# Run sums of a graph kernel copied out of their PSUM banks by ScalarE into four SBUF places, and added from there by VectorE one unit later

## The reference, cut to what matters

```python
h = gelu(x @ W_pre + b_pre)
aggr = segment_sum(h[src] * edge_attr, dst)      # layer 0: gather, weigh, sum by node
x1 = x + aggr
y = gelu(gelu(x1 @ W1 + b1) @ W2 + b2)
x2 = layernorm(x + x1 + y)

t = x2 @ W_lin.T + b_lin                         # layer 1: the same edges, no edge weights
agg = segment_sum(t[src] * dinv[src] * dinv[dst], dst)
out = layernorm(x2 + relu(agg + x2 @ W_root.T + b_root))
```

## Time and profile before

| | |
|---|---|
| three runs | 1155.4, 1145.21, 1153.62 us (median 1153.62) |
| profiled execution | 1145.42 us, span of the trace 1143.6 us |
| busy share PE, DVE, ACT, POOL | 82%, 64%, 44%, 73% |
| mean granted TensorE clock | 0.91 of full speed |

### The profile page before, as it was taken

How to read it: one execution, slowest core, us unless ns; L and a number is a source line. 1 busy time by engine, 2 the same in 40 slices (tenths; PEclk the granted TensorE clock), 3 DMA queues, 4 the chain that set the end, 5 groups by cost and what they waited for, 6 DMA issues and landing times. The chain is left out here.

```text
span 1143.6 us, 20856 instructions
## 1 busy us (share of the span) xinstructions
PE 934.5 (82%) x7455; PEld 811.1 (71%) x7455; DVE 737.3 (64%) x1442; ACT 499.6 (44%) x846; POOL 839.2 (73%) x915
## 2 busy tenths in 40 slices
PE   6744776667667966888989999989999999799796
PEld 6643544444445844776888888789999989698696
DVE  8177987676777677668657858734435465556655
ACT  2303876566755675567557666541001010001116
POOL 7787777777777777777777777777777777777603
PEclk9866987778877988999999999999999999899898
DMA  8542876567666768788899899979998888677734
GB/s 226 158 116 61 301 264 217 188 197 244 193 201 196 241 220 277 219 272 291 267 288 280 252 319 304 300 228 288 275 262 267 253 255 246 183 198 193 183 84 96
DMA packets 185668, 260.24 MB, mean 228 GB/s; under 512 B 68600, under 2 KB 163832, under 8 KB 178968
## 3 DMA queue, kind: packets, MB, share of 16 engines
q1 hardware_dynamic: 158278, 215.57, 58.6%
q0 software_dynamic: 26992, 42.82, 15.9%
q10 hardware_dynamic: 290, 0.45, 0.2%
HBM read 173.12 MB, written 85.62 MB: 226 GB/s over the span
## 5 line engine op out<-in xcount | busy, mean ns | idle before, releaser
L855 POOL DMA_INDIRECT gath<-table_h,srcs x791 | 781.6, 988 | 241.2 <-issue 239.3
L1494 PE MATMUL bank_q<-piece_raw,early_late 128*96 128x250 bf16 x3453 | 407.4, 272 | 7.6 <-issue 3.2
L1494 PEld LDWEIGHTS bank_q<-piece_raw,early_late 128*96 128x96 bf16 x3453 | 380.2, 124 | 12.4 <-issue 5.1
L944 ACT CAST counts_raw<-bank_q 128x490 bf16<-128x490 f32 x400 | 279.6, 756 | 153.3 <-PE bank_q L1472 149.9
L1440 PE MATMUL seg<-onehot,msg 128*97 128x128 f32 (+1 forms) x1662 | 237.0, 296 | 69.5 <-DVE msg L1244 40.4
L1440 PEld LDWEIGHTS seg<-onehot,msg 128*97 128x97 f32 x1662 | 214.5, 183 | 85.5 <-issue 58.7
L1472 PE MATMUL bank_q<-hots_raw 128*128 128x245 bf16 x834 | 161.3, 289 | 49.9 <-ACT counts_raw L944 33.5
L1342 DVE TENSOR_TENSOR hots_raw<-counters,kb 128x1960 bf16<-128x1960 bf16 (+1 forms) x157 | 182.3, 1161 | 0.0
L944 ACT CAST counts_raw<-bank_b 128x490 bf16<-128x490 f32 x200 | 151.4, 757 | 69.3 <-PE bank_b L1472 66.7
L1244 DVE TENSOR_TENSOR msg<-gath,edg 128x480 f32<-128x480 f32 x166 | 108.1, 651 | 96.2 <-DMA gath<-table_h,srcs 87.1
L1472 PEld LDWEIGHTS bank_q<-hots_raw 128*128 128x128 bf16 x834 | 70.7, 103 | 112.9 <-ACT counts_raw L944 69.0
(11 more groups left out here) (196 smaller groups left out, 623.4 us busy)
## 6 DMA issues: line engine op xcount, KB each, us to landing
counts_hbm<-counts_raw SPq DMA_DIRECT2D x50, 1531.2 KB
piece_raw<-counts_hbm SPq DMA_DIRECT2D x250, 250.0 KB
edg<-in_edge SPq DMA_DIRECT2D x166, 240.0 KB
gath<-table_h,srcs POOLq DMA_INDIRECT x791
piece_raw<-counts_hbm SPq DMA_DIRECT2D x38, 125.0 KB
piece_raw<-counts_hbm SPq DMA_DIRECT2D x25, 187.5 KB
counts_raw<-counts_hbm SPq DMA_DIRECT2D x4, 625.0 KB, 5.9
gath<-x_hbm SPq DMA_DIRECT2D x10, 234.4 KB
```

Source lines behind the costliest of these rows:

```text
L855: pool.indirect_dma_start(gath[0:k, u % GS * UT + j, :], None, table[0], bass.IndirectOffsetOnAxis(ap=srcs[0:k, t:t + 1], axis=0)).then_in ...
L944: act.copy(counts[:, k % 2, :, i * WD:(i + 2) * WD].rearrange("p a (w n) -> p w a n", w=2), counted).then_inc(s_kept, 1)
L1494: mm = pe.matmul(sums(r)[0:D, 0:DN], parts[:, FINE[c] + i, part, :], rows, start=(first and i == 0 and part == 0), stop=(last and i == til ...
```

## The change

ScalarE gets a new item `keep`, put right behind the last piece of each run: it waits for the run's last piece and copies the 96x250 sums from the bank into one of four SBUF places `run_sums` (a place is free again when the `dense` of four runs before is done). `begin_run` now waits for that copy (`s_run_kept`) instead of for `dense`. `dense` takes its input from `run_sums`; it is put one unit later (`u - 1`), and up to four runs may wait when a new one begins. In the building stage a new run may begin while others wait. The pieces are the same 313; there are 171 runs instead of 170.

```diff
 def schedule():
         if last:
+            order.append(("keep", r))
             waiting.append((u, r))
     def flush(u):
-        while waiting and waiting[0][0] < u:
+        while waiting and waiting[0][0] < u - 1:
             order.append(("dense", waiting.pop(0)[1]))
     def next_piece(u, least):
-                while len(waiting) > 2:
+                while len(waiting) >= KS:
                     order.append(("dense", waiting.pop(0)[1]))
...
-                if open_run or not (waiting and u <= built + 1):
-                    next_piece(u, next(n for until, n in LEAST if u < until))
+                next_piece(u, next(n for until, n in LEAST if u < until))
...
+        run_sums = sb("run_sums", [D, KS, DN])
...
+            def keep_run(r):
+                act.wait_ge(s_used, runs[r][1] + 1)
+                if r >= KS:
+                    act.wait_ge(s_dense, r - KS + 1)
+                act.copy(run_sums[:, r % KS, :], sums(r)[0:D, 0:DN]).then_inc(s_run_kept, 1)
...
             def dense(r):
-                run_sum = sums(r)[0:D, 0:DN]
+                run_sum = run_sums[:, r % KS, :]
...
-                dve.wait_ge(s_used, q + 1)
+                dve.wait_ge(s_run_kept, r + 1)
...
             def begin_run(r):
                 if run_before(r) is not None:
-                    pe.wait_ge(s_dense, run_before(r) + 1)
+                    pe.wait_ge(s_run_kept, run_before(r) + 1)
```

More of the change, by code:

```diff
@@ L61 @@
 LATER = 1
+KS = 4
 ZS = 4
@@ L456, in build @@
         s_dense = sem("s_dense")
+        s_run_kept = sem("s_run_kept")
         s_taken = sem("s_taken")
@@ L990, in _ @@
                 what = item[0]
+                if what == "keep":
+                    keep_run(item[1])
                 if what == "meta":
@@ L1345, in dense @@
             def dense(r):
-                e, q, is_apart, takes = runs[r]
-                run_sum = sums(r)[0:D, 0:DN]
+                e, _, is_apart, takes = runs[r]
+                run_sum = run_sums[:, r % KS, :]
                 high = upper[:, (e - SPLIT) * DN:(e - SPLIT) * DN + DN] if e >= SPLIT else None
```

## The result

The changed kernel takes 1157.13 us (median of 19 runs, 1151.41 to 1164.4), the kernel before 1148.88 us (19 runs, 1140.82 to 1155.4) on the same chip. The ratio is 1.0084, 95% interval [1.0063, 1.0104]: the change costs 9.6 us, 0.84%. The forecast was 6.3 us or 0.5% slower, "same" within 1%. It gave 1160 us, but from a base of 1153.62 us, the median of three runs; with 19 runs that base is 1148.88 us. So 1160 lies near 1157.13 partly by luck, and the difference of 9.6 us is what has to be explained. Sign and size class came out; the reason came out in part only, and the following is mostly about that.

What follows compares the result with a forecast made beforehand. GpSimd's chain of gathers was taken to bound the kernel. Adds 6.0 us plus copies 0.3, all else 0, gave 6.3 us on 1153.62: 1160 us, range 1150 to 1171 (the forecast case's own 1157 to 1164).

Steps and rivals of the forecast that it cites:

- GpSimd's chain sets the pace: From 110 to 1083 us GpSimd goes from gather to gather, one each 1.28 us; slack at unit 112 is 14.9 us.
- The keeps in the building stage: ScalarE's copies there make TensorE 2 to 12 us late by unit 112; the slack covers it, so 0.
- The adds: 133 dense before unit 162 become adds with two SBUF inputs that delay GpSimd's gathers: 6.0 us, bounds 0 and 16.9.
- The 0.045: Gather delay in us per two-SBUF add, from three hits, 0.49 us together, among 11 L1360 adds before the last gather.
- The rule for an instruction at random: Gather delay from a VectorE instruction of length d: (d - 0.12)^2 / 2.56, giving 0.034 us for 0.416 us.
- The 13 copies: Dense that are copies (L1364, 0.414 us from PSUM) become copies inside SBUF; at half of L1360's price, 0.3 us.
- The tail: Behind unit 162's gathers: chunk 12's t some 1 us earlier, four additions about 2 us later; together 0, bounds -3.6 and +1.5.
- The step that failed: Chunk 12's first step gains three adds (1.8 us); the Gelu's table load behind a keep gives most of that back.
- are hidden in its idle time: After the building stage ScalarE has little to do, so its copies of run sums there cost nothing.
- The last four additions: At the end, four additions stand behind the last add; the last chunk and step1 wait for them, about 2 us.
- 77.4 us from message 162 to the end, within 2: Check set beforehand: unit 162's message to the end of the span stays 77.4 us; if it moves, the prediction is wrong.

Runs made afterwards that it cites:

- The experiment with the adds alone: Kernel before, with dense reading an SBUF tile of zeros in place of the bank, same waits and order: 1148.55 us against 1146.84, ratio 1.0022.

## Why the prediction was right or wrong

**GpSimd's chain sets the pace, and the copies don't stop it.** Right. Its waits for messages are 2.1 us, and the message of unit 112 is earlier: it ends at 761.22 + 0.65 = 761.9 us, its room is needed at 785.48, so the slack grew from 14.9 to 23.6 us. The smallest of all units is now 21.4 us.

**The keeps in the building stage: 0.** Right, and by the reason given. TensorE's new waits for a copy are 6.3 us in 18 cases, the longest 1.4, where 2 to 12 us were worked out; VectorE's waits for pieces are gone, and the kernel with the copies up to unit 150 is 1.0012.

**The adds: 6.0 us.** The mechanism was right, the term too large, by two times or more. The experiment with the adds alone gives 2.5 us (0.5 to 4.7), and the gathers that start under an add run 2.2 us over in its trace and 2.1 in that of the changed kernel, 0.015 us an add, not 0.045. The 0.045 was three hits among eleven. The rule for an instruction at random, 0.034, lay nearer but was too large too; why the adds meet fewer starts than at random is open. *The 13 copies: 0.3 us.* Inside SBUF they take 0.29 us on average and not 0.41; they lengthen two gathers, by 0.02 and 0.06 us.

**The tail: 0, bounds -3.6 and +1.5.** Wrong, and here most of the loss is: 7.9 us by the kernel that copies only from unit 150 on. The step that failed reads "ScalarE's table load before that chunk's Gelu now stands behind a keep, which gives most of that back". It priced one load in one place as less than 1.8 us, where chunk 12's first Gelu comes 3.6 us later behind its product. It left out that the copy itself waits (2.06 us for its piece), that the load before the square root stands behind a copy too, and that chunk 11 has the same two loads and passes its lateness on to message 162. The same holds for its sentence that behind the building stage the copies "are hidden in its idle time". The bound above was worked out from VectorE's additions alone; it should have held the loads, 1.28 us in the four places of chunks 11 and 12, 5.1 us, with the copies' waits on top (one of the four, the square root's in chunk 12, then turned out not to be on the way).

**The last four additions: about 2 us.** The 1.1 us more of TensorE's idle time is there, but taking two thirds of it away (1.67 us left) gives nothing that can be measured.

**"77.4 us from message 162 to the end, within 2".** It is 88.9, and by the prediction's own words that makes it wrong in its reason. Not all of the 11.5 us are the change's, though. The last rows of the table above say 4.6 of them lie in the last 50 us, and there TensorE's clock was low. The 8 us from the last chunk's first step (stretch, PE busy and its products, then PEclk, DMA share and GB/s), in the kernel before, in the changed one, and in the kernel before with its loads early:

```profile
1097.38:1105.38 8.00, 7.80 (x95) 1.00 0.44 111
```

```profile
1108.12:1116.12 8.00, 7.87 (x41) 0.53 0.31 70
```

```profile
1099.48:1107.48 8.00, 7.93 (x49) 0.58 0.43 97
```

The third kernel has no copies at all, its TensorE idles the same 1.27 us ahead of the turning, its median is that of the kernel before, and yet this execution shows the clock of the changed one and 50.9 us to the end, as there. So the low clock there does not need the copies; it costs some 4.7 us. Set beside this execution, the changed kernel's is 8.5 us longer: 1.2 up to the gathers' end, 2.1 - 2.1 around the message, 6.1 on chunk 12's way, 1.4 behind it, -0.1 in the last 51 us.

Does the change make the low clock more frequent? Each kernel was profiled once, but over the kernels at the usual times the traces lean that way: the clock in these 8 us is 0.52 to 0.58 in all six with copies in the tail, and 1.00 in four of the five without. If it does, up to 4.7 of the 9.6 us could be the clock's, and no run here settles it. It takes nothing from the loads: the traces of both kernels that pull them forward show the low clock too, and their times are still 7 us under the others'.

**The sum.** 2.5 us of adds and 7.9 us of tail are 10.4 against the 9.6 measured (the adds of the tail, some 38 of 133, are in both). The forecast's 6.3 was near it by luck: a term at least twice too large stood in for one that was missing.

## What to carry to other kernels

An engine with "little to do" still walks a list in order: before handing it short copies, look at what stands behind each copy's wait, and count table loads, which sit directly ahead of the activation that needs them and slide behind anything put in between. If such copies must go there, pull the load ahead of them with a one-element activation of the next kind. And when a term comes from one profile, look first at how much traces differ without it: here the gathers' sums of kernels without the new adds differed by 2.8 us, more than the 1.8 us between before and after, and an execution with the low clock was 4.7 us longer in its last 51 us.

## What the runs showed of the hardware

- VectorE adds with both inputs in SBUF hold back a GpSimd indirect gather that starts under them, by what is left of them less 0.12 us; the new adds of 0.417 us cost 0.015 us each on average by the gathers that start under them, whereas of 58 gathers that start under a copy by ScalarE (0.363 us, from PSUM to SBUF) only 6 took over 1.0 us, each of them with a VectorE instruction whose inputs are all in SBUF at or just behind its start.
- TensorE's granted clock in the last chunk stayed at 1.00 (2.4 GHz) in one execution and was at 1.2 GHz for most of 8 us (mean 0.58) in one of nearly the same kernel, with the same 1.27 us of idle time ahead of it; 4.7 us of difference.
- The kernel before took 1147 us in three comparisons and 1618 us in a fourth; there the gathers of nearly the same kernel took the same 0.94 us, but GpSimd waited 475.7 us for messages.
- A table load of 1.28 us started 0.02 us behind the copy ahead of it, and the activation that needed it 0.01 us behind the load; an activation of one element (0.20 us) of the next kind pulls it forward.
